# One batch's statistics and scales ahead of another's positions and row transfers, and two TensorE groups ahead of their turn, in a dense block followed by a mixture of experts

## The reference

```python
x = x + _L0_attn_ref(_layernorm(x), ...)   # x1 = conv(LN(.)) + .;  silu(LN(x1) @ w1 + b1) @ w2 + b2 + x1
x = x + _L0_ffn_ref(_layernorm(x), ...)

# _L0_ffn_ref, for each token
logits = jnp.einsum('th,eh->te', x, router_w)
topk_logits, topk_idx = jax.lax.top_k(logits, K)          # K = 2 of E = 8
probs = jax.nn.softmax(topk_logits, axis=-1)
hmid = jax.nn.gelu(jnp.einsum('th,efh->etf', x, w1) + b1[:, None, :])
y = jnp.einsum('etf,ehf->eth', hmid, w2) + b2[:, None, :]
out = jnp.einsum('eth,te->th', y, combine)
```

## Time and profile before

| | |
|---|---|
| device time, median of 3 runs | 444.3 us (443.93 to 446.59) |
| profiled execution | 446.09 us, of which its span is 444.3 |
| TensorE, busy share of the span | 85% |
| VectorE | 79% |
| ScalarE | 72% |
| GpSimd | 61% |
| granted TensorE clock, mean of the span | 0.942 of full speed |

### The profile page before, as it was taken

One profiled execution on the slowest core, in us unless ns is written; L12 is line 12 of the kernel. 1 busy time (PEld: TensorE's weight loads), 2 busy tenths in 40 slices (PEclk: granted clock), 3 DMA queues, 4 the chain that ended last, 5 costly groups with the idle time before them and its releaser, 6 DMA issues.

```text
span 444.3 us, 11234 instructions
## 1 busy us (share of the span) xinstructions
PE 376.9 (85%) x2723; PEld 321.1 (72%) x2723; DVE 349.3 (79%) x1332; ACT 319.5 (72%) x772; POOL 271.5 (61%) x339
## 2 busy tenths in 40 slices
PE   1173288797999999989979899999999999999970
PEld 1131257484867768666748899899999999999970
DVE  7999999798899989897652777887677777777770
ACT  4792586978889798689544786677777777777740
POOL 6890955645687798756483376477654555545451
PEclk9996589998989898999997999999999999999995
DMA  7649222110222221231323243444433333333200
GB/s 247 188 144 321 83 49 48 29 20 14 48 89 47 89 62 50 70 93 51 90 86 115 59 143 113 120 147 131 115 92 94 104 102 102 107 100 109 70 3 0
DMA packets 34434, 41.60 MB, mean 94 GB/s; under 512 B 5382, under 2 KB 29459, under 8 KB 34244
## 3 DMA queue, kind: packets, MB, share of 16 engines
q1 hardware_dynamic: 27236, 23.56, 18.4%
q0 software_dynamic: 7136, 17.33, 13.5%
HBM read 19.52 MB, written 18.92 MB: 86 GB/s over the span
## 4 chain that ended last, share of the span: by engine, by line
PE 55%; POOL 13%; DVE 11%; ACT 6%; issue 6%; POOLq 0%; DVEq 0%; ACTq 0%
PE up_p L1057 12%; PE down_p L1076 12%; PE down_p L876 8%; POOL sorted_rows L584 6%; PE turn_p L1057 5%; PE turn_p L1076 5%; PE up_p L865 5%; PE turn_p L853 3%; PE up_p L1066 2%; ACT work L674 2%; POOL scale L549 2%; PE route_p L918 2%; DVE stats L1158 1%; ACT rows L688 1%; ACT work L681 1%
## 5 line engine op out<-in xcount | busy, mean ns | idle before, releaser
L620 POOL DMA_INDIRECT out<-result,out_id x91 | 89.4, 983 | 68.1 <-DVE result L1564 47.2
L584 POOL DMA_INDIRECT sorted_rows<-rows,pos x64 | 71.8, 1122 | 37.6 <-issue 27.2
L865 PE MATMUL up_p<-h_t,work 128*128 128x512 f32 x128 | 67.7, 653 | 9.4 <-ACT work L648 8.1
L1057 PE MATMUL up_p<-xt,work 128*128 128x128 f32 x520 | 69.4, 277 | 0.6 <-ACT hid_t L806 0.5
L876 PEld LDWEIGHTS down_p<-w_sb,work 128*128 128x128 f32 x512 | 62.2, 196 | 9.9 <-issue 9.3
L1076 PE MATMUL down_p<-mw_sb,hid_t 128*128 x520 | 69.1, 276 | 0.1
L821 ACT ACTIVATE work<-mw_c 128x256 f32 x182 | 65.8, 416 | 0.3 <-issue 0.2
L876 PE MATMUL down_p<-w_sb,work 128*128 128x128 f32 x512 | 64.5, 281 | 0.1
L1057 PEld LDWEIGHTS up_p<-xt,work 128*128 128x128 f32 x520 | 63.2, 192 | 1.2 <-issue 1.1
L1076 PEld LDWEIGHTS down_p<-mw_sb,hid_t 128*128 128x128 f32 x520 | 63.3, 192 | 0.6 <-issue 0.5
L806 ACT ACTIVATE hid_t<-up_p 128x512 f32<-128x512 f32 x65 | 38.8, 597 | 29.8 <-PE up_p L1057 29.6
(11 more groups left out here) (248 smaller groups left out, 744.2 us busy)
## 6 DMA issues: line engine op xcount, KB each, us to landing
tin<-sorted_rows SPq DMA_DIRECT2D x91, 136.0 KB, 2.2
resid<-in_x SPq DMA_DIRECT2D x8, 512.0 KB, 3.8
resid<-work POOLq DMA_DIRECT2D x8, 512.0 KB, 4.7
sorted_rows<-zeros SPq DMA_DIRECT2D x29, 136.0 KB, 2.4
out<-result,out_id POOLq DMA_INDIRECT x91, 2.3
work<-in_mw SPq DMA_DIRECT2D x1, 1024.0 KB, 6.3
sorted_rows<-rows,pos POOLq DMA_INDIRECT x64, 2.5
work<-in_w SPq DMA_DIRECT2D x1, 256.0 KB
```

The lines of the kernel that those rows point to most:

```text
L584: g.indirect_dma_start(sorted_dram, bass.IndirectOffsetOnAxis(pos[b % 2][:, j:j + 1], 0), rows[b % ROWBUFS][:, j, :], None).then_inc(s_sor ...
L620: g.indirect_dma_start(out_rows, bass.IndirectOffsetOnAxis(out_id[k][:, :], 0), result[k][:, :], None, bounds_check=TOKENS - 1, oob_is_err ...
L865: t.matmul(dst, w1_g[:, k], half(h_t, h), start=True, stop=True).then_inc(s_up, 1)
L1057: last = t.matmul(mid_banks[bank_of(s)][:, c * TILE:(c + 1) * TILE], ring[s % RING][:, c * 128:(c + 1) * 128], xt[s % DEEP][:, :], start=T ...
```

## The change

In the last dense batch VectorE takes the statistics of x2 of batch 6 ahead of the positions of batch 5. GpSimd makes the scales of batch 6 ahead of all eight row transfers of batch 5, where two of them came first. TensorE multiplies down group 1 of batch 7 ahead of the transpose of batch 6, and up group 3 ahead of the router product of batch 6.

```diff
@@ GpSimd
             for i in range(LAST):
                 iteration(i)
 
-            sort_rows(LAST - 2, range(0, 2))
             x2_scales(LAST - 1)
-            sort_rows(LAST - 2, range(2, TPB))
+            sort_rows(LAST - 2, range(TPB))
             x2_scales(LAST)
@@ TensorE
             tile_sums(0)
             mlp_up(LAST, 2)
             tile_facts(0)
+            mlp_down(LAST, 1)
             xm_turn(LAST - 1)
-            mlp_down(LAST, 1)
+            mlp_up(LAST, 3)
             route(LAST - 1)
-            mlp_up(LAST, 3)
             mlp_down(LAST, 2)
             mlp_down(LAST, 3)
             place(LAST - 1)
@@ VectorE
             pair_facts()
             choose(LAST - 2)
             x2_sum(LAST - 1)
+            x2_stats(LAST - 1)
             positions(LAST - 2)
-            x2_stats(LAST - 1)
             tile_numbers(0)
             tile_windows(0)
             tile_table(0)
```

## The result

| | before | changed |
|---|---|---|
| device time, median | 446.63 us (443.93 to 447.65, 6 runs) | 442.35 us (440.99 to 444.73, 6 runs) |
| ratio to before | | 0.990, 95% interval 0.9855 to 0.9945 |
| profiled execution | 446.09 us, span 444.3 | 444.73 us, span 443.0 |

A second set of runs gave 0.990 again (0.9865 to 0.9935). The change wins 1%, 4.3 us in the medians; the interval leaves 2.5 to 6.5 us, so it lies on both sides of the 1% border.

The account below looks back on a forecast made before the run. It took TensorE's 3.13 us wait for batch 6's normalised x2 and the halved clock behind it as the loss; x_copy(0) moving from 247.38 to 242.9 gains 4.5 us, so 444.3 - 4.5 = 439.8 us, own range 439.2 to 440.5.

Parts of the forecast that it names:

- the stated 438.8 to 442.6: Whole kernel: wider time range in us, taking in the forecast, the later-gate rival and the clock rival.
- two rivals which did not come: Later first-tile gate, 441.0 us, chance 10 in 100; clock falling at new idle bits, 442.5 us, chance 8 in 100.
- Statistics 224.05 worked out: VectorE: batch 6's statistics, moved ahead of batch 5's positions, end at 224.05 us, 2.15 us sooner.
- the same pieces in another order, all ready in time, end at the same 237.88: GpSimd: reordered scales and batch 5 rows still end at 237.88 us, give or take 0.1; first tile load stays at 240.14.
- a sign of being wrong: First tile load, SyncE: the forecast counts as wrong if this load moves from 240.14 us.
- 236.85: VectorE: choose(6) begins at 236.85 us, 4.0 us sooner, following route(6) by 0.10 us.
- The decomposition: TensorE: 3.13 idle plus 1.10 and 1.63 lost clock, less 0.15 slip and 1.72 up group, makes choose(6) 4.0 us sooner.
- my first rival: Later gate at the first tile: scales come no sooner or first loads land late; gain 3.3, 441.0 us, chance 10 in 100.
- ScalarE's chain: Before the first tile's copy: tanh through third ring copy ends at 242.85 us, the latest of three gates.
- the load: Before the first tile's copy: load issued at 240.14, landed and turned by 242.5 to 242.8 us.
- the chance of 8 in 100: TensorE: clock falls at new idle bits, costing 2.7 us, time 442.5 us; chance 8 in 100.
- No loss in the tile stage: First tile's copy to end: stage keeps its 196.9 us; rival that it gives all back, 444 us, chance 4 in 100.

Follow-up runs that it names:

- e6: Against e2: GpSimd's three waits for batch 5's rows put ahead of the scales; 25.71 us from the last h_t copy to the first tile's copy (e2 26.24).
- e5: Kernel before plus 24 useless identity transposes on TensorE in its 3.13 us wait; 27.86 us from the last h_t copy to the first tile's copy (before 30.45).
- e1: Kernel before with only TensorE's order changed, VectorE and GpSimd as before; ratio 0.9937 (0.9907 to 0.9967).
- e2: Changed kernel with TensorE's order put back to that of before, VectorE and GpSimd as changed; ratio 0.995 (0.9921 to 0.998).
- e8: Against e7: gelu table and third ring copy ahead of batch 6's probabilities, first tile's turn ahead of place(6); ratio 0.9924 (0.9891 to 0.9957).
- again: Second execution of the changed kernel, nothing altered, beside e8; ratio to before 0.990 (0.9865 to 0.9935).
- e6_timed: Second execution of e6, timed, nothing altered; ratio to before 0.9918 (0.9882 to 0.9955).
- e7: Against e6: ScalarE's probabilities of batch 4 ahead of its xm copy of batch 5; 44.26 us from batch 6's h_t copy to first tile's copy (e6 44.16).
- e9: Against e8: GpSimd's wait for batch 5's positions put behind the scales again; 43.84 us from batch 6's h_t copy to first tile's copy (e8 44.40).

## Why the prediction was right

The forecast was 4.5 us of gain; the traces have 4.27 and the medians 4.3. The mechanism was the forecast one. That the medians agree with the traces to 0.1 us is luck, as their interval spans 4 us. Off its base of 444.3 the gain gives 440; the measured median is 442.35, since more runs of before put its own median at 446.63. The three runs that I took the base from were 2.3 us low. So the time misses the forecast's own 439.2 to 440.5 and lies inside the stated 438.8 to 442.6 by 0.25 us, in a part that was there for two rivals which did not come: that too is luck. (By its own terms, 439.8 + 0.4 + 0.2, the forecast's own range ends at 440.4.)

*VectorE.* Statistics 224.05 worked out, 224.09 found; positions 224.9 and 224.90; tile_counts(0) 0.17 us late, at 228.07 - 3.02 = 225.05, where I had 0.15. Right.

*GpSimd.* The scales at 225.40, as worked out. The step that failed in part is the end of the rows: "the same pieces in another order, all ready in time, end at the same 237.88". They ended at 240.35 + 0.96 - 3.02 = 238.29. The pieces were the same, but not what stands between them: 0.55 us ahead of the first row instead of 0.17, as e6 showed by putting it back. The trace of before had the other case as well: where rows follow scales with their waits between them, ahead of the rows of batch 6, its GpSimd timeline has

```profile
252.78 0.20 POOL L575 TENSOR_TENSOR shift<-tmp,scale 128x8 f32<-128x8 f32 x1
253.52 1.04 POOL L584 DMA_INDIRECT sorted_rows<-rows,pos  x1 [0.55 <-issue]
```

and I had taken alone. The first load moved with it, from 240.14 to 240.56, which the prediction had named as a sign of being wrong; it cost little only because the next gate was as late.

*TensorE.* Down, turn, up, route without a break, at full clock; choose(6) at 237.01 against 236.85. The 0.16 us are in the down group, which took 1.89 and not 1.78, and in the step from route's start to choose's, 1.95 and not 1.85. The decomposition (3.13 of wait and 2.7 of clock, less 1.72 for the up group) is confirmed in its parts: e5 took the clock alone and got 2.6; e1 took TensorE's order alone and got 3.3, the very sum of my first rival, which had the scales come no sooner. All of these are set against one execution of before, in which the clock fell. The medians of the timed runs give less than the traces in all five later sets: 3.1 us for e1 (3.3 in the trace), 3.1 for e2 (4.2), 3.4 for e8 (4.2 to the end), 3.4 for e6 (4.6), 4.1 for the changed kernel again (4.3). That would fit a fall of the clock at 230 us that comes in some executions of before and not in others; it isn't shown, and the spread of the runs is as large.

*The gates.* I had ScalarE's chain last, at 242.85, the load at 242.5 to 242.8. Found: the third ring copy ended at 245.32 + 0.71 - 3.02 = 243.01 and the first turn, for which TensorE stood until the tile was there, began at 242.77 and was copied at 243.11. In this execution the load was last, by 0.1 us; in the second one (`again`) the ring copy ended at 243.68 and the turn at 243.67 of its own clock, so the two gates tie. That the first turn stood for the load is read from the distance: 2.21 us from issue to turn, the time to landing in the earlier trace rows, while the bracket names only `issue`. For the time this makes 0.1 us; for what each edit is worth it makes a great difference. With both of TensorE's edits taken back (e2), choose(6) and ScalarE's chain behind it come 1.27 us sooner, and x_copy(0) does not. The change consists of two ways of closing one gap, worth 3.3 and 4.2 us alone and 4.3 together, by the traces.

*The rivals.* No clock loss at the new waits of 0.65 and 0.41 us: 1.00 in all stretches from 220 to 250 us, in this execution and in `again`. The prediction's argument for it was one row, the turn at 194.37; the same trace has a turn at 125.88 that took 1.56 us behind a wait of 0.34 (last section), so the chance of 8 in 100 was less well founded than it looks. No loss in the tile stage: 196.9 to 197.0 us in all kernels that keep its order.

## What to carry to other kernels

A wait of TensorE costs its length and, in some executions, a slow stretch behind it, so filling it with ready work of its own can bring most of the gain without the late result coming sooner (3.28 of 4.27 us here). When several edits close the same gap, take each back by itself: the sum of their separate gains (3.3 + 4.2 us) says nothing of the whole (4.3). Where a sum ends with three gates within 0.4 us of each other, work each out down to its last semaphore wait, since which of them is last decides what is worth changing next.

## What the runs showed of the hardware

**One wait, three prices.** The time between executions of one kernel is spread by 2.7 to 7 us within a set of runs (before: 443.2 to 449.8 us in all its runs), and the traces show one place where it arises. In batch 2's dense work TensorE waits 2.64 us in every trace, and in most of them the clock is low behind it. Busy time and clock by stretches, before:

```profile
106.00:108.00 2.00, 1.73 (x2) 0.73 (x3) 1.76 (x12) 1.37 (x3) 1.59 (x3) 0.50 0.02 4
108.00:110.00 2.00, 2.00 (x10) 1.65 (x9) 1.83 (x9) 0.90 (x2) 1.62 (x5) 0.68 0.00 0
110.00:112.00 2.00, 2.00 (x17) 1.67 (x16) 1.97 (x12) 2.00 (x4) 1.84 (x4) 1.00 0.86 164
```

in the changed kernel, whose code is the same there:

```profile
106.00:108.00 2.00, 1.75 (x2) 0.73 (x3) 1.76 (x12) 1.34 (x3) 1.62 (x3) 0.50 0.01 4
108.00:110.00 2.00, 2.00 (x10) 1.55 (x8) 1.83 (x9) 0.69 (x1) 1.62 (x5) 0.50 0.00 0
110.00:112.00 2.00, 2.00 (x7) 1.35 (x7) 1.97 (x12) 1.94 (x4) 1.85 (x4) 0.50 0.85 164
112.00:116.00 4.00, 4.00 (x16) 3.35 (x16) 2.68 (x11) 2.34 (x7) 2.11 (x2) 0.52 0.29 53
```

and in e8, again with the same code:

```profile
100.00:120.00 20.00, 17.36 (x106) 12.37 (x106) 17.43 (x77) 18.96 (x45) 12.32 (x15) 1.00 0.14 28
```

The clock came back before 110 us in the first, only towards 116 in the second, and never fell in the third. ScalarE's h_t copies of batches 2 and 3, which lie on either side of the wait, stand 25.42 us apart in the first, 28.50 in the second and 23.95 in the third; the first two differ by the 3.0 us of the section on the result. Of the twelve profiles of this study five have 23.95 us and the clock at 1.00 (e2, e6_timed, e7, e8, e9), six have 25.4 to 25.5, and one, the changed kernel's, 28.5. A longer wait of 2.98 us, in batch 1, left the clock at 1.00 in eleven of the twelve; in e2 it fell, and the copies of batches 1 and 2 stand 26.20 us apart instead of 23.01. The h_t copy of batch 6 stands at 196.8 to 201.5 us over the twelve, and no kernel has an edit ahead of it. So the price of the slow stretch at 233 us in the earlier trace rows, 2.7 us, is that of one execution of before; in others it may be less, nothing at all, or more, which no run here measured apart. Nor does a fall need a long wait just ahead of it: in batch 3, before, the clock was 0.59 over 126 to 128 us behind a wait of 0.34 us, and in e7 it was 1.00 in the same place. There it cost nothing (24.05 and 24.06 us between the h_t copies of batches 3 and 4), because TensorE waited for ScalarE anyway, for 0.45 us in the one and 2.14 in the other. The Trainium skill (TensorE: Matmul & The Clock Gate, Part 1: The HAM clock gate) says of the first matmuls of a kernel that how many of them run at the low clock varies from run to run. The traces show the same in the middle of one.

**Full clock behind a filled gap.** With the 24 transposes of e5 the granted clock stood at 1.00 over the stretch that had 0.50 before. That the transposes did it is likely but not shown, as in other executions the clock stayed at 1.00 behind waits of 2.64 and 2.98 us without them.

**No drain behind the table load.** In the changed kernel too the load of the gelu table took 1.28 us (243.91 to 245.19), and ScalarE's next instruction began at 245.21; in the earlier trace rows the ring copy follows as closely. The further 1.38 us that the Trainium skill names (ScalarE: Activation LUTs, What ACT_TABLE_LOAD costs) did not show.
